# A two-stage kernel whose second stage gets its transposed rows by DMA, and whose first stage transposes the next tile one chunk earlier

## The chip, the cores and the metric

The kernel runs on one core of a Trainium2 chip. The metric is the time of one execution on the device, in microseconds (us). Five engines work side by side, each through its own queue of instructions in order: TensorE (PE: matmuls; its weight loads are listed as PEld), VectorE (DVE), ScalarE (ACT), GpSimd (POOL) and SyncE (SP). SyncE and ScalarE issue the transfers of this kernel, which 16 DMA engines carry out. Engines wait for each other by semaphores alone.

## What is computed

x has 2 x 1024 rows of 2048 values, ctx has 2 x 2048 rows of 2048 values.

```python
def fake_quant(x, s, z):                    # xattn: rounds to 0..255
    q = clip(round(x / s + z), 0, 255)
    return (q - z) * s
x = x + tanh(g_xattn) * matmul(fake_quant(layernorm(x)), fake_quant(ctx))      # per batch, 1024x2048 @ 2048x2048
y = layernorm(x)
logits = y @ gate_w.T + expert_bias         # 4 experts
one_hot = one_hot(argmax(logits))
z = y @ lora_A.T                            # 4 experts x 8
delta = z of the chosen expert @ lora_B.T
x = x + tanh(g_ffn) * (y @ W_up.T + delta)
```

## The kernel before

The 2048 rows are 16 tiles of 128 rows. A tile is 128 x 2048 in float32, 1 MB. Two stages follow each other on TensorE.

**First stage.** For each tile t: VectorE's `moments` (line 545) and `quant_scale`, ScalarE's `sqrt` (line 352), then ScalarE's `quant` rounds the normalised tile to int16 into one of two buffers `q1` in HL (line 358), and VectorE's `clip` (line 592) makes exact bfloat16 of it. TensorE transposes it in 16 blocks of 128 x 128 (`transposes`, line 853) into two PSUM banks TR, and ScalarE's `evac` copies both out to `q1T` (line 377); for tiles 0 to 3 VectorE copies the second half. Then come four chunks of 512 columns, each of 16 matmuls (`chunk`, line 875), and VectorE adds each chunk to the rows (`epi`, line 599). Tiles 0 to 3 go through chunk by chunk together, tiles 4 to 15 one by one. The transposes of tile t + 1 stand behind chunk 1 of tile t, that is its second. ctx arrives as 32 tiles; ScalarE rounds each (`ctx_round`, line 385), VectorE clips it (`ctx_clip`, line 609). Tiles 8 to 15 use ctx tiles 16 to 31.

The order of work on ScalarE and VectorE is written out by hand in `period(p, a, b, c)`, one call for each tile from 4 on. On ScalarE a period is: a, `sqrt(p + 2)`, b, `quant(p + 2)`, `evac(p + 1)`, c. In periods 4 to 7 the pieces a, b and c round one ctx tile each; from period 8 on they are absolute sums of a tile of W (`abs_sum`, line 394) and high halves of it (`w_high`, line 403). VectorE's period has `epi` of the last chunk of tile p - 1, `moments(p + 2)`, a, `epi`, `quant_scale(p + 2)`, `epi`, b, `clip(p + 2)`, `epi`, c. There, a, b and c are `ctx_clip`, later the powers of two of W (`w_pow`, line 617) and the low halves (`w_low`, line 629). SyncE's queue holds the loads and the stores in one written order: `store(t)` waits for `epi` of the last chunk of tile t, `row(u)` waits for the store that frees its buffer, and the loads of ctx and W wait for the buffers that they fill.

**Second stage.** W_up with the gates and lora_A beside it is 2084 columns wide and is kept in SBUF as two float16 halves; each row of it (a partition's columns of the k-th tile) is scaled by its own power of two. y, the normalised tile, is split into two float16 halves as well: VectorE's `norm` writes it in float32 to T (line 588), ScalarE's `y_high` rounds it to HL[:, 0] (line 413), and VectorE's `y_low` puts the rest in HL[:, 1] (line 636). HL holds one tile. TensorE transposes the two halves in 32 blocks, in four groups (`y_transposes`, line 912), VectorE multiplies each group by the column scales `wback` on its way out of PSUM into YT, the transposed tile, which has two buffers (`yT_out`, line 645). A tile's product (`tile2`) is five chunks of 416 to 418 columns, 48 matmuls each (line 920), with an addition for lora_B at the end of each (line 927) and a small transpose for z behind the second chunk (line 934). In the middle of tile s stand the transposes of tile s + 1: groups 0 and 1 ahead of chunk 3, groups 2 and 3 ahead of chunk 4. VectorE's order for a tile is `route(s)` (line 659 on), `moments`, `norm`, `y_low` of tile s + 1, then `epi2(s, c)` (line 693) with the four `yT_out` of tile s + 1 among them. ScalarE's is the store of tile s - 1 (line 424), `z_out(s)` (line 419), `sqrt` and `y_high` of tile s + 1. SyncE loads the rows that were put away in the first stage.

Of the kernel before, what the change touches and what calls it, by code (L numbers as in the profile page):

```python
# [7 lines left out]
ALU = mybir.AluOpType  # L8
# [3 lines left out]
P = 128  # L12
# [6 lines left out]
def build(nc, x, ctx, w, b_t, scal, out):  # L19
# [17 lines left out]
    KEEP = 4  # L37
    HALF = KT // 2
# [7 lines left out]
    o_t = out.rearrange("(t p) d -> t p d", p=P)  # L46
    h_t = nc.dram_tensor("h_scratch", (TILES - KEEP, P, D), F32).ap()

# [7 lines left out]
    with es:  # L56
# [12 lines left out]
        YT = sb("rows_T", [P, 2, KT, 2, P], F16)  # L69
# [4 lines left out]
        Braw = S1[0:ZR, 0:D]  # L74
        arena_bf = arena[:, :].bitcast(BF16)
        arena_i16 = arena[:, :].bitcast(I16)
        q1T = YT[:, :, :, :, :].rearrange("p a k h m -> p (a k h m)").bitcast(BF16).rearrange(
# [99 lines left out]
        s_yh = sem("y_high"); s_yl = sem("y_low"); s_yt = sem("yT_group"); s_ye = sem("yT_out")  # L177
        s_m2 = sem("chunk2_done"); s_dl = sem("delta_done"); s_rt = sem("route_step"); s_zs = sem("z_stack_ready")
# [36 lines left out]
        def _(sp):  # L215
# [111 lines left out]
            for s in range(KEEP + 1, TILES):  # L327
                row(TILES + s)
# [18 lines left out]
        def _(act):  # L347
# [57 lines left out]
            def y_high(s):  # L405
                act.wait_ge(s_norm, s + 1)
                if s == 0:
                    act.wait_ge(s_tr, 2 * TILES)
                else:
                    act.wait_ge(s_yt, 4 * s)  # L410
                    act.wait_ge(s_yl, s)
                u = TILES + s
                A(HL[:, 0, :], Xt(u), ACT.Identity, bias=L(u, "nmr"), scale=L(u, "rstd")).then_inc(s_yh, 1)  # L413
# [21 lines left out]
            ctx_round(0)  # L435
            evac(0)
            ctx_round(1)
            sqrt(1)
            ctx_round(2)
            quant(1)  # L440
# [25 lines left out]
            def period(p, a, b, c):  # L466
# [37 lines left out]
        def _(dve):  # L504
# [67 lines left out]
            def norm(s):  # L572
# [15 lines left out]
                v.tensor_scalar(T[:, 0:D], Xt(u), L(u, "mean"), L(u, "rstd"), ALU.subtract, ALU.mult).then_inc(s_norm, 1)  # L588
# [43 lines left out]
            def y_low(s):  # L632
                dve.wait_ge(s_yh, s + 1)
                if s >= 1:
                    dve.wait_ge(s_yt, 4 * s)
                v.tensor_tensor(HL[:, 1, :], T[:, 0:D], HL[:, 0, :], ALU.subtract).then_inc(s_yl, 1)  # L636

            def yT_out(s, g):
# [3 lines left out]
                src = TR[g % 2].bitcast(F16).rearrange("p (a m) -> p a m", a=4)  # L642
                dst = YT[:, s % 2, 4 * g:4 * g + 4].rearrange("p k h m -> p k (h m)")
                back = wc[:, 4 * g:4 * g + 4].unsqueeze(2).to_broadcast([P, 4, 2 * P])
# [152 lines left out]
            step(v.tensor_scalar(wc[:, :], wp[:, :], V["rPM"], None, ALU.mult))  # L797
            step(v.tensor_scalar(V["sc2"], V["PM"], UN, None, ALU.mult))
# [21 lines left out]
            for s in range(1, TILES):  # L820
# [5 lines left out]
                for c in range(3):  # L826
                    epi2(s, c)
                for g in range(4):
                    if g == 2:
                        epi2(s, 3)  # L830
                    if s + 1 < TILES:
                        yT_out(s + 1, g)
                epi2(s, 4)

        @block.tensor
        def _(pe):
# [46 lines left out]
            def stage1(slow):  # L883
# [19 lines left out]
            def y_transposes(s, g):  # L903
# [6 lines left out]
                for i in range(8):  # L910
                    k, h = 4 * g + i // 2, i % 2
# [4 lines left out]
            def products(s, c, kts, first):  # L916
                a, b = CUT[c], CUT[c + 1]
                for kt in kts:
                    for yh, wh in ((0, 0), (0, 1), (1, 0)):
                        mm = mmul(bank[c][:, 0:b - a], YT[:, s % 2, kt, yh, :], W(kt, wh, a, b),  # L920
# [18 lines left out]
            def tile2(s):  # L939
                nxt = s + 1 < TILES  # L940
                pe.wait_ge(s_ye, 4 * s + 4)
# [8 lines left out]
                if nxt:  # L950
                    y_transposes(s + 1, 0)
                    y_transposes(s + 1, 1)
# [3 lines left out]
                if nxt:  # L956
                    y_transposes(s + 1, 2)
                    y_transposes(s + 1, 3)
# [66 lines left out]
```

## Time and profile before

| what | value |
|---|---|
| median of 3 runs | 1028.18 us |
| runs | 1027.31 to 1029.14 us |
| profiled execution, its own time | 1028.02 us |
| its span, first to last instruction | 1026.2 us |
| TensorE busy | 972.0 us (95%) |
| VectorE busy | 460.6 us (45%) |
| ScalarE busy | 230.3 us (22%) |
| mean granted TensorE clock | 0.99 of full speed |

The span is the time between the first and the last instruction in the trace; the rest of the execution lies around it. Busy shares are averages over both stages. Matmuls are pipelined and their ends are modelled, so the distance between two starts is a better measure than the duration of a row.

### The profile page before, as it was taken

How to read it: one execution, taken by the hardware profiler on the slowest of the kernel's cores; microseconds unless marked ns; L12 is line 12 of the kernel's file. 1: busy time of each engine (PE TensorE's matmuls, PEld its weight loads, DVE VectorE, ACT ScalarE, POOL GpSimd, SP SyncE). 2: the span in 40 equal slices, each digit the busy share in tenths (PEclk: the TensorE clock that was granted, in tenths of full speed). 3: DMA queues.
4: the chain of work that ended last, by engine and by line, in shares of the span. 5: the costliest groups of instructions: out<-in, count | busy, mean ns of one | idle time of the engine just before them, and what ended most of it. 6: DMA issues, size and time to landing. Idle time of an engine off the chain costs nothing.

```text
span 1026.2 us, 13127 instructions
## 1 busy us (share of the span) xinstructions
PE 972.0 (95%) x5728; PEld 531.3 (52%) x5728; DVE 460.6 (45%) x885; ACT 230.3 (22%) x192; POOL 2.3 (0%) x16
## 2 busy tenths in 40 slices
PE   2899799899899999999999999999999999999997
PEld 1444344444355555555555555555555555555554
DVE  6764565766577542342534233252424325242401
ACT  6584657575633000000000000000000000000000
POOL 0000000000000000000000000000000000000000
PEclk9999999999899999999999999999999999999999
DMA  9968967677534202021020202112020210101011
GB/s 373 420 240 328 402 259 274 200 246 289 221 139 143 82 1 83 1 82 61 22 82 1 83 1 82 42 42 82 2 82 1 82 42 1 42 1 42 1 42 42
DMA packets 16445, 119.57 MB, mean 117 GB/s; under 512 B 1952, under 2 KB 1952, under 8 KB 1952
## 3 DMA queue, kind: packets, MB, share of 16 engines
q1 hardware_dynamic: 14080, 101.90, 26.1%
q10 hardware_dynamic: 2304, 16.78, 4.0%
q8 instruction: 48, 0.79, 0.3%
q14 instruction: 13, 0.11, 0.0%
HBM read 89.31 MB, written 29.36 MB: 116 GB/s over the span
## 4 chain that ended last, share of the span: by engine, by line
PE 74%; DMA 11%; ACT 5%; DVE 5%; issue 3%; SPq 1%; ACTq 0%; DVEq 0%
PE bank L920 62%; PE bank L875 7%; PE bank L912 3%; DMA arena<-in_ctx 2%; ACT arena L385 2%; DMA rows<-in_x 2%; DMA normed<-in_w 2%; DMA h_scratch<-rows 2%; DVE arena L629 2%; DMA stage<-in_ctx 1%; DMA stage<-in_w 1%; PE bank L927 1%; ACT rows_T L377 1%; DVE bn L545 1%; ACT halves L358 1%
## 5 line engine op out<-in xcount | busy, mean ns | idle before, releaser
L920 PE MATMUL bank<-arena,rows_T 128*128 128x416 f16 (+1 forms) x3840 | 686.6, 339 | 2.2 <-DVE arena L629 1.2
L920 PEld LDWEIGHTS bank<-arena,rows_T 128*128 128x128 f16 x3840 | 370.6, 97 | 300.5 <-issue 4.6
L875 PE MATMUL bank<-arena,rows_T 128*128 128x512 bf16 x1024 | 235.5, 390 | 30.2 <-ACT rows_T L377 18.4
L875 PEld LDWEIGHTS bank<-arena,rows_T 128*128 128x128 bf16 x1024 | 100.7, 100 | 157.6 <-issue 21.0
L693 DVE SCALAR_TENSOR_TENSOR rows<-bank,derived,rows 128x416 f32<-128x416 f32 (+2 forms) x80 | 48.4, 641 | 228.9 <-PE bank L927 228.9
L419 ACT ACTIVATE z_stack_T<-bank 96x128 fp32r<-96x128 f32 x16 | 4.4, 274 | 600.7 <-PE bank L934 600.7
L545 DVE BATCH_NORM_STATS2 bn<-rows 128x6 f32<-128x512 f32 x124 | 76.5, 680 | 10.7 <-DMA rows<-in_x 8.6
L645 DVE TENSOR_TENSOR rows_T<-bank,wback 128x1024 f16<-128x1024 f16 x64 | 75.0, 1216 | 0.2 <-DVE z_stack L675 0.2
L659 DVE SCALAR_TENSOR_TENSOR route<-bank,derived,scal 128x4 f32<-128x4 f32 x16 | 3.5, 221 | 115.9 <-PE bank L920 115.8
L599 DVE SCALAR_TENSOR_TENSOR rows<-bank,derived,rows 128x512 f32<-128x512 f32 x60 | 44.4, 747 | 20.9 <-PE bank L875 20.8
L636 DVE TENSOR_TENSOR halves<-normed,halves 128x2048 f16<-128x2048 f32 x16 | 36.7, 2292 | 30.3 <-ACT halves L413 30.3
L385 ACT ACTIVATE arena<-arena,scal,derived 128x2048 int16<-128x2048 f32 x22 | 45.2, 2084 | 10.2 <-DMA arena<-in_ctx 10.2
L413 ACT ACTIVATE halves<-rows,ln 128x2048 f16<-128x2048 f32 x16 | 33.5, 2095 | 39.7 <-DVE normed L588 39.7
L609 DVE TENSOR_SCALAR arena<-arena,derived 128x2048 bf16<-128x2048 int16 x32 | 24.0, 750 | 37.0 <-ACT arena L385 37.0
L554 DVE RECIPROCAL ln<-ln 128x1 f32<-128x1 f32 x32 | 5.1, 160 | 66.3 <-ACT ln L352 66.3
L912 PE MATMUL bank<-ident_h,halves 128*128 128x128 f16 x512 | 34.3, 220 | 0.2 <-DVE rows_T L645 0.2
L358 ACT ACTIVATE halves<-rows,ln 128x2048 int16<-128x2048 f32 x15 | 31.3, 2087 | 4.8 <-DVE ln L569 4.8
L912 PEld LDWEIGHTS bank<-ident_h,halves 128*128 128x128 f16 x512 | 29.0, 98 | 6.2 <-issue 5.0
L853 PE MATMUL bank<-ident_bf,halves 128*128 128x128 bf16 x256 | 17.7, 225 | 15.2 <-DVE halves L592 15.2
L629 DVE SCALAR_TENSOR_TENSOR arena<-stage,wscale,arena 128x2084 f16<-128x2084 f32 x11 | 26.1, 2384 | 8.3 <-ACT arena L403 8.2
L927 PE MATMUL bank<-b_stack,z_stack_T 96*128 96x416 f32 (+2 forms) x80 | 29.1, 432 | 0.4 <-ACT z_stack_T L419 0.4
L377 ACT ACTIVATE rows_T<-bank 128x1024 bf16<-128x1024 bf16 x28 | 27.1, 1010 | 8.9 <-PE bank L853 8.9
(82 smaller groups left out, 271.9 us busy)
## 6 DMA issues: line engine op xcount, KB each, us to landing
arena<-in_ctx SPq DMA_DIRECT2D x22, 1024.0 KB, 17.7
stage<-in_w SPq DMA_DIRECT2D x17, 1042.0 KB, 6.2
out<-rows ACTq DMA_DIRECT2D x16, 1024.0 KB, 3.9
rows<-in_x SPq DMA_DIRECT2D x15, 1024.0 KB, 9.9
rows<-h_scratch SPq DMA_DIRECT2D x12, 1024.0 KB, 4.8
h_scratch<-rows SPq DMA_DIRECT2D x11, 1024.0 KB, 8.3
stage<-in_ctx SPq DMA_DIRECT2D x10, 1024.0 KB, 10.4
normed<-in_w SPq DMA_DIRECT2D x7, 1042.0 KB, 6.6
```

What stands on the lines that cost most here:

```text
L358: A(q1_i16(t), Xt(t), ACT.Relu, bias=L(t, "qb"), scale=L(t, "qs")).then_inc(s_qi, 1)
L377: A(q1T[:, t % 4, GROUP * g:GROUP * (g + 1), :].rearrange("p k m -> p (k m)"), TR[g].bitcast(BF16), ACT.Copy).then_inc(s_ev, 1)
L385: A(Qc(c, True), buf, ACT.Relu, bias=z2, scale=V["rs2"]).then_inc(s_cr, 1)
L545: v.bn_stats(bn[:, u % 2, i, :], Xc(u, i * 512, (i + 1) * 512)).then_inc(s_bn, 1)
L599: v.scalar_tensor_tensor(out=xs, in0=bank[ROT[g % 6]][:, :], scalar=V["coef"], in1=xs, op0=ALU.mult, op1=ALU.add).then_inc(s_epi, 1)
L629: v.scalar_tensor_tensor(out=W(n, 1), in0=wbuf[k][:, :], scalar=wa[:, n:n + 1], in1=W(n, 0), op0=ALU.mult, op1=ALU.subtract).then_inc(s_lo, 1)
L645: v.tensor_tensor(dst, src, back, ALU.mult).then_inc(s_ye, 1)
L693: v.scalar_tensor_tensor(out=xs, in0=bank[c][:, a - CUT[c]:b - CUT[c]], scalar=V["gs"], in1=xs, op0=ALU.mult, op1=ALU.add).then_inc(s_e2, 1)
L875: mm = mmul(bk, q1T[:, t % 4, kt, :], Q(b, n, kt), start=(kt == 0), stop=(kt == KT - 1 and not slow), skip_group_check=slow)
L912: mm = nc.tensor.transpose(TR[g % 2].bitcast(F16)[:, i * P:(i + 1) * P], HL[:, h, k * P:(k + 1) * P], idh[:, :])
L920: mm = mmul(bank[c][:, 0:b - a], YT[:, s % 2, kt, yh, :], W(kt, wh, a, b), start=(first and kt == kts[0] and yh == 0 and wh == 0), stop=False,
L927: mmul(bank[c][:, a - CUT[c]:b - CUT[c]], zT[:, :].bitcast(F32R), Bst[:, a - EXT:b - EXT], start=False, stop=True, skip_group_check=True). ...
```

## The change

In the second stage tiles 0 and 1 (`BY_PE = 2`) keep TensorE's transposes. Tiles 2 to 15 are transposed by one DMA each, SBUF to SBUF, that SyncE issues: both halves of HL, 128 x 4096 float16, into YT, whose layout is now half, k, row. It waits for the low half of the tile and for the products of tile s - 2, which used the same half of YT. `y_high` of the tile after waits for this transfer instead of the transposes, since it overwrites HL. The column scales were applied on the way out of PSUM; now they are applied ahead of the split, by a row WR that holds all 2048 of them in every partition. SyncE writes the 128 x 16 scales `wback` to memory and loads them back to all partitions into S0. `norm` multiplies by WR in place of the row's rstd, which `y_high` and `y_low` multiply in. The loads of rows 5 on for this stage now alternate with the transfers in SyncE's queue.

In the first stage the transposes of tile t + 1 stand behind chunk 0 of tile t in place of chunk 1, for tiles from 4 on. ScalarE's period is: a, `sqrt(p + 2)`, `evac(p + 1)`, `quant(p + 2)`, b, c. In the head of the program `sqrt(1)` and `quant(1)` come one place earlier.

```diff
+            for s in range(BY_PE, TILES):
+                if s + 3 < TILES:
+                    row(TILES + s + 3)
+                sp.wait_ge(s_yl, s + 1)
+                sp.wait_ge(s_m2, 5 * (s - 1))
+                sp.dma_start_transpose(YT[:, s % 2].rearrange("p h k m -> p (h k) m"),
+                                       HL[:, :, :].rearrange("p h d -> p (h d)")).then_inc(s_dt, 16)
...
+            sp.wait_ge(s_wc, 1)
+            sp.dma_start(wrow_d.rearrange("k p -> p k"), wc[:, :],
+                         allow_slow_non_contiguous=True).then_inc(s_wr0, 16)
+            sp.wait_ge(s_wr0, 16)
+            sp.wait_ge(s_lo, KT)
+            sp.dma_start(WR, wrow_d.rearrange("k p -> (k p)").unsqueeze(0).to_broadcast([P, D])).then_inc(s_wr, 16)
...
-                b()
+                evac(p + 1)
                 if p + 2 < TILES:
                     quant(p + 2)
-                evac(p + 1)
+                b()
                 c()
...
+                    dve.wait_ge(s_wr, 16)
+                    v.scalar_tensor_tensor(out=T[:, 0:D], in0=Xt(u), scalar=L(u, "mean"), in1=WR, op0=ALU.subtract,
+                                           op1=ALU.mult).then_inc(s_norm, 1)
...
+                    v.scalar_tensor_tensor(out=HL[:, 1, :], in0=T[:, 0:D], scalar=L(TILES + s, "rstd"), in1=HL[:, 0, :],
+                                           op0=ALU.mult, op1=ALU.subtract).then_inc(s_yl, 1)
...
-                        if n == 1 and t + 1 < TILES:
+                        if n == 0 and t + 1 < TILES:
                             transposes(t + 1)
...
-                pe.wait_ge(s_ye, 4 * s + 4)
+                if s < BY_PE:
+                    pe.wait_ge(s_ye, 4 * s + 4)
+                else:
+                    pe.wait_ge(s_dt, 16 * (s - BY_PE + 1))
...
-                if nxt:
-                    y_transposes(s + 1, 0)
-                    y_transposes(s + 1, 1)
                 free2(s, 3)
```

TensorE's queue over one tile of the second stage, from its first chunk to the next tile's, stands like this before:

```order
L920 MATMUL bank<-arena,rows_T 128x416 x96
L934 MATMUL bank<-ident_f,z_stack 96x128
L920 MATMUL bank<-arena,rows_T 128x416 x48
L927 MATMUL bank<-b_stack,z_stack_T 128x380
L927 MATMUL bank<-b_stack,z_stack_T 128x416 x2
L912 MATMUL bank<-ident_h,halves 128x128 x16
L920 MATMUL bank<-arena,rows_T 128x418 x48
L927 MATMUL bank<-b_stack,z_stack_T 128x418
L912 MATMUL bank<-ident_h,halves 128x128 x16
L920 MATMUL bank<-arena,rows_T 128x418 x48
L927 MATMUL bank<-b_stack,z_stack_T 128x418
```

and like this after, where line 920 has become 946, 927 has become 953 and 934 has become 960:

```order
L946 MATMUL bank<-arena,rows_T 128x416 x96
L960 MATMUL bank<-ident_f,z_stack 96x128
L946 MATMUL bank<-arena,rows_T 128x416 x48
L953 MATMUL bank<-b_stack,z_stack_T 128x380
L953 MATMUL bank<-b_stack,z_stack_T 128x416 x2
L946 MATMUL bank<-arena,rows_T 128x418 x48
L953 MATMUL bank<-b_stack,z_stack_T 128x418
L946 MATMUL bank<-arena,rows_T 128x418 x48
L953 MATMUL bank<-b_stack,z_stack_T 128x418
```

Both blocks of 16 transposes are gone from the tile; nothing else moved. SyncE's queue behind the last load of W stands like this after the change (`stage1` is where B lands, `stage0` is WR):

```order
L331 DMA stage1<-in_b_t 96x2048
L333 DMA w_back_row<-wback 128x16x1
L337 DMA stage0<-w_back_row 128x2048
L229 DMA rows<-h_scratch 128x2048
L343 DMA_TRANSPOSE rows_T<-halves 128x32x128
```

Before, the load of B is followed by the loads of rows alone; now the two transfers of the scales stand between, and each load of rows but for the last ones is followed by one transposing transfer. In the first stage, ScalarE's queue from the copy of tile 5 (period 4) to that of tile 6 (period 5) stands like this before (`rows_T` is the copy out of PSUM, `arena` a ctx tile rounded, `ln` the square root, `halves` the x tile rounded; what is left out is a branch that isn't taken):

```order
L377 ACTIVATE rows_T<-bank 128x1024 x2
L385 ACTIVATE arena<-arena,scal,derived 128x2048 x2
L352 ACTIVATE ln<-ln 128x1
L385 ACTIVATE arena<-stage,scal,derived 128x2048
L358 ACTIVATE halves<-rows,ln 128x2048
...
L377 ACTIVATE rows_T<-bank 128x1024 x2
```

and after, with 377 become 393, 385 become 401, 352 become 368 and 358 become 374:

```order
L393 ACTIVATE rows_T<-bank 128x1024 x2
L374 ACTIVATE halves<-rows,ln 128x2048
...
L401 ACTIVATE arena<-stage,scal,derived 128x2048
L401 ACTIVATE arena<-arena,scal,derived 128x2048 x2
L368 ACTIVATE ln<-ln 128x1
L393 ACTIVATE rows_T<-bank 128x1024 x2
```

The copy of tile 6 stood behind the ctx tile of operation b (the one from `stage`) and the rounding of tile 7; now it is ahead of both.

## Rows read from the trace of the kernel before

**Rows 1.** The page's chain that ended last, shares of the span by line

```profile
PE bank L920 62%; PE bank L875 7%; PE bank L912 3%; DMA arena<-in_ctx 2%; ACT arena L385 2%; DMA rows<-in_x 2%; DMA normed<-in_w 2%; DMA h_scratch<-rows 2%; DVE arena L629 2%; DMA stage<-in_ctx 1%; DMA stage<-in_w 1%; PE bank L927 1%; ACT rows_T L377 1%; DVE bn L545 1%; ACT halves L358 1%
```

**Rows 2.** Timeline of one second-stage tile: start us, duration us, engine, line, operation, [idle before]

```profile
615.38 17.05 PE L920 MATMUL bank<-arena,rows_T 128*128 128x416 f16 x96
...
620.13 0.32 SPq L224 DMA_DIRECT2D rows<-h_scratch  x1
...
634.01 1.35 DVE L588 TENSOR_SCALAR normed<-rows,ln 128x2048 f32<-128x2048 f32 x1
...
637.52 2.29 DVE L636 TENSOR_TENSOR halves<-normed,halves 128x2048 f16<-128x2048 f32 x1 [2.16 <-ACT halves L413]
...
641.38 1.07 PE L912 MATMUL bank<-ident_h,halves 128*128 128x128 f16 x16
...
642.28 8.64 PE L920 MATMUL bank<-arena,rows_T 128*128 128x418 f16 x48
...
651.86 8.66 PE L920 MATMUL bank<-arena,rows_T 128*128 128x418 f16 x48
...
660.55 0.70 PE L920 MATMUL bank<-arena,rows_T 128*128 128x416 f16 x3
```

**Rows 3.** Timeline of TensorE in the last tile, fourth and fifth chunk

```profile
1002.71 8.65 PE L920 MATMUL bank<-arena,rows_T 128*128 128x418 f16 x48
...
1011.40 8.67 PE L920 MATMUL bank<-arena,rows_T 128*128 128x418 f16 x48
```

**Rows 4.** The page's groups: count | busy us, mean ns | idle before, releaser

```profile
L875 PE MATMUL bank<-arena,rows_T 128*128 128x512 bf16 x1024 | 235.5, 390 | 30.2 <-ACT rows_T L377 18.4 <-DVE arena L609 7.4 <-DVE rows_T L604 4.4
...
L629 DVE SCALAR_TENSOR_TENSOR arena<-stage,wscale,arena 128x2084 f16<-128x2084 f32 x11 | 26.1, 2384 | 8.3 <-ACT arena L403 8.2
```

**Rows 5.** Timeline of TensorE in the first stage

```profile
107.64 8.75 PE L875 MATMUL bank<-arena,rows_T 128*128 128x512 bf16 x32 [2.25 <-ACT rows_T L377]
...
127.42 8.75 PE L875 MATMUL bank<-arena,rows_T 128*128 128x512 bf16 x32 [3.23 <-ACT rows_T L377]
...
195.62 8.75 PE L875 MATMUL bank<-arena,rows_T 128*128 128x512 bf16 x32 [3.56 <-ACT rows_T L377]
...
262.37 9.88 PE L875 MATMUL bank<-arena,rows_T 128*128 128x512 bf16 x32 [4.05 <-ACT rows_T L377]
...
272.98 13.98 PE L875 MATMUL bank<-arena,rows_T 128*128 128x512 bf16 x64
```

**Rows 6.** DMA view: a queue's packets, MB, share; issues with KB and us to landing

```profile
q1 hardware_dynamic: 14080, 101.90, 26.1%
...
out<-rows ACTq DMA_DIRECT2D x16, 1024.0 KB, 3.9
...
rows<-h_scratch SPq DMA_DIRECT2D x12, 1024.0 KB, 4.8
...
scal<-in_scal SPq DMA_DIRECT2D x1, 5.0 KB, 1.6
```

**Rows 7.** Timeline: the load of B, and the high half of tile 2

```profile
324.77 0.34 SPq L326 DMA_DIRECT2D stage<-in_b_t  x1
...
364.38 2.10 ACT L413 ACTIVATE halves<-rows,ln 128x2048 f16<-128x2048 f32 x1 [2.44 <-DVE normed L588]
```

**Rows 8.** Timeline of ScalarE in the first stage

```profile
121.38 2.10 ACT L385 ACTIVATE arena<-stage,scal,derived 128x2048 int16<-128x2048 f32 x1 [5.20 <-DMA stage<-in_ctx]
...
125.36 1.91 ACT L377 ACTIVATE rows_T<-bank 128x1024 bf16<-128x1024 bf16 x2
...
139.61 2.10 ACT L385 ACTIVATE arena<-arena,scal,derived 128x2048 int16<-128x2048 f32 x1 [5.80 <-DMA arena<-in_ctx]
...
200.36 1.94 ACT L394 ACTIVATE arena<-stage 128x2084 f32<-128x2084 f32 x1 [2.96 <-DMA stage<-in_w]
...
235.46 1.94 ACT L394 ACTIVATE stage<-stage 128x2084 f32<-128x2084 f32 x1 [4.73 <-DMA stage<-in_w]
```

**Rows 9.** Chain that ended last, in order of time: start us, us, what

```profile
183.78 8.35 DMA h_scratch<-rows
```

More of the change, by code:

```diff
@@ L37, in build @@
     KEEP = 4
+    BY_PE = 2
     HALF = KT // 2
@@ L408, in y_high @@
                     act.wait_ge(s_tr, 2 * TILES)
-                else:
+                elif s <= BY_PE:
                     act.wait_ge(s_yt, 4 * s)
                     act.wait_ge(s_yl, s)
+                else:
+                    act.wait_ge(s_dt, 16 * (s - BY_PE))
                 u = TILES + s
-                A(HL[:, 0, :], Xt(u), ACT.Identity, bias=L(u, "nmr"), scale=L(u, "rstd")).then_inc(s_yh, 1)
+                if s < BY_PE:
+                    A(HL[:, 0, :], Xt(u), ACT.Identity, bias=L(u, "nmr"), scale=L(u, "rstd")).then_inc(s_yh, 1)
+                else:
+                    A(HL[:, 0, :], T[:, 0:D], ACT.Identity, scale=L(u, "rstd")).then_inc(s_yh, 1)
             def z_out(s):
@@ L587, in norm @@
                     dve.wait_ge(s_bst, 2)
-                v.tensor_scalar(T[:, 0:D], Xt(u), L(u, "mean"), L(u, "rstd"), ALU.subtract, ALU.mult).then_inc(s_norm, 1)
+                if s < BY_PE:
+                    v.tensor_scalar(T[:, 0:D], Xt(u), L(u, "mean"), L(u, "rstd"), ALU.subtract,
+                                    ALU.mult).then_inc(s_norm, 1)
+                else:
+                    dve.wait_ge(s_wr, 16)
+                    v.scalar_tensor_tensor(out=T[:, 0:D], in0=Xt(u), scalar=L(u, "mean"), in1=WR, op0=ALU.subtract,
+                                           op1=ALU.mult).then_inc(s_norm, 1)
             def clip(t):
@@ L633, in y_low @@
                 dve.wait_ge(s_yh, s + 1)
-                if s >= 1:
-                    dve.wait_ge(s_yt, 4 * s)
-                v.tensor_tensor(HL[:, 1, :], T[:, 0:D], HL[:, 0, :], ALU.subtract).then_inc(s_yl, 1)
+                if s < BY_PE:
+                    if s >= 1:
+                        dve.wait_ge(s_yt, 4 * s)
+                    v.tensor_tensor(HL[:, 1, :], T[:, 0:D], HL[:, 0, :], ALU.subtract).then_inc(s_yl, 1)
+                else:
+                    v.scalar_tensor_tensor(out=HL[:, 1, :], in0=T[:, 0:D], scalar=L(TILES + s, "rstd"), in1=HL[:, 0, :],
+                                           op0=ALU.mult, op1=ALU.subtract).then_inc(s_yl, 1)
             def yT_out(s, g):
@@ L641, in yT_out @@
                     dve.wait_ge(s_mm, place[(13 if s == 0 else 15, NCH - 1)] + 1)
-                src = TR[g % 2].bitcast(F16).rearrange("p (a m) -> p a m", a=4)
-                dst = YT[:, s % 2, 4 * g:4 * g + 4].rearrange("p k h m -> p k (h m)")
-                back = wc[:, 4 * g:4 * g + 4].unsqueeze(2).to_broadcast([P, 4, 2 * P])
+                src = TR[g % 2].bitcast(F16).rearrange("p (h a m) -> p h a m", h=2, a=4)
+                dst = YT[:, s % 2, :, 4 * g:4 * g + 4, :]
+                back = wc[:, 4 * g:4 * g + 4].unsqueeze(1).unsqueeze(3).to_broadcast([P, 2, 4, P])
                 v.tensor_tensor(dst, src, back, ALU.mult).then_inc(s_ye, 1)
@@ L825, in _ @@
                     y_low(s + 1)
-                for c in range(3):
+                for c in range(5):
                     epi2(s, c)
[L828 to L833, printed above, removed]
         @block.tensor
@@ L939, in tile2 @@
             def tile2(s):
-                nxt = s + 1 < TILES
-                pe.wait_ge(s_ye, 4 * s + 4)
+                if s < BY_PE:
+                    pe.wait_ge(s_ye, 4 * s + 4)
+                else:
+                    pe.wait_ge(s_dt, 16 * (s - BY_PE + 1))
                 for c in range(3):
```

22 lines of the change are left out of this document (11 added, 11 removed).

## The prediction

> **What bounds the kernel now.** I read the chain of waits first [rows 1]. Line 920, TensorE's products in the second stage, carries 62% of the span, and no other line more than 7. So I read that stage at the size of one tile [rows 2]: the first product of a tile starts at 615.38, that of the next at 660.55, 45.17 us later, and between them TensorE is never idle. Within the tile there are two blocks of 16 transposes (line 912). The next products start 0.90 us after each block does (641.38 to 642.28 for the first). The last tile has no such block [rows 3]: from its fourth chunk to its fifth 8.69 us pass (1002.71 to 1011.40), against 9.58 in [rows 2] (642.28 to 651.86), so a block costs 0.89 to 0.90 us of the path. The first stage is another matter [rows 4, 5]: TensorE sits idle for 30.2 us before line 875, 18.4 of them until line 377, ScalarE's copy of the transposes out of PSUM, in eight waits. [Rows 5] has the four longest, 2.25, 3.23, 3.56 and 4.05; the others are 1.68, 1.97, 0.16 and 1.55. Behind the four the next 32 matmuls take 8.75 us (three times) or 9.88, where half of the 64 in 13.98 us is 7.0, and 7.07 stands behind the shorter waits: the granted clock falls to the lower of its levels (1.2 of 2.4 GHz) for a while after such a wait. That adds 3 x 1.68 + 2.81 = 7.85 us. 18.4 + 7.85 = 26.3 us is thus all that a perfect first-stage order could return.
>
> **Second stage, what goes.** Tiles 2 to 15, 14 of them, are transposed by DMA; their 28 blocks leave TensorE: 28 x 0.90 = 25.2 us. VectorE loses its copies out of PSUM too, but it has idle time and doesn't set the end. Nothing else on TensorE's path changes, if the transposed tile has landed when the next tile starts.
>
> **Second stage, what comes.** That condition is the heart of the forecast. One buffer of halves holds the tile, so its transfer starts only after the low half (line 636), and must end before the next tile starts. In [rows 2] the low half starts at 637.52 and takes 2.29: it ends 639.81, 24.4 us into the tile. Two edits shift this. Line 588 becomes an operation with two tensor inputs, since it multiplies by the row of scales: line 629 does such an operation on 2084 columns in 2.38 us [rows 4], so 2048 take 2.34 where now 1.35 stand, 1.0 us more. The low half becomes the same kind, 2.34 instead of 2.29. So the transfer is released 25.5 us into a tile, and the tile lasts 45.17 - 1.80 = 43.37 us. The slack is 43.37 - 25.5 = 17.9 us. In SyncE's queue the load of rows for tile s + 3 is ahead of it, and waits for the store of tile s - 2. Such a load is issued at 620.13 in [rows 2], 4.8 us into the tile and as soon as the store has landed, so 20 us before the transfer is released. Both megabytes are through by then, and the transfer has the DMA engines to itself.
>
> How long it takes no row shows. Nearest by bytes are the loads and stores of 1 MB in this stage, 4.8 and 3.9 us [rows 6]. By pieces it could be far worse: the SP queue moved 14080 packets of 7.2 KB in 26.1% of 16 engines' time, 0.304 us each; a transposed megabyte falls into 32 blocks x 128 rows = 4096 pieces of 256 bytes, and if each cost as much as such a packet it would take 4096 x 0.304 / 16 = 78 us. The price lies between 4 and 78 us. I take it as under 17.9, because a plain megabyte needs 4.8 and the slack is 3.7 times that, while the piece bound charges 256 bytes like 7.2 KB. Then it costs nothing, and TensorE covers it. If the cover is gone, each microsecond above 17.9 is paid 14 times, as the release of the next transfer moves with the start of its tile.
>
> The Trainium skill, Advanced Engine Details and Errata, section X-Bar Transpose (TRN2), says that such transfers are as fast as plain ones, 350 to 400 GB/s: an estimate of 3 us for this megabyte, and the sum would be the same.
>
> **The row of scales.** The column scales go out to memory as 2048 single values and come back to all partitions. SyncE issues both behind the load of B, which it issues at 324.77, and the first user is the norm of tile 2, just before the high half at 364.38 [rows 7]: both moments move alike. That is 39 us for two transfers. If each of the 2048 values cost a packet's 0.304 us the first would take 39 us and the second some 5, a lateness of 5 us that the slack of tile 2 mostly takes. I take zero, 0 to 5.
>
> **First stage.** On TensorE the transposes of tile t + 1 come one chunk earlier; on ScalarE their copy comes ahead of rounding the next x tile (line 358) and of operation b of the period. Up to tile 8 operation b rounds a ctx tile that has just landed. [Rows 8] show the present order: b starts at 121.38, when its load has landed, rounding follows it, the copy is third at 125.36, and TensorE starts at 127.42 [rows 5]. Each of the next loads waits for a store of the tile before, so this is a loop. Landings in it are at 121.38 and 139.61, 18.2 us apart. The two operations that come out of it from behind b, 2.0 for rounding (as for b, 125.36 - 121.38 for both) and 1.9 for the copy, leave 18.2 - 3.9 = 14.3, less than TensorE's own tile: four chunks in 13.98 [rows 5] and 0.90 for the transposes, 14.9 us. So for tiles 5 to 8 TensorE becomes the bound, and the waits before them go: 2.25 + 3.23 + 1.68 + 1.97 = 9.1 us and 2 x 1.68 of slow clock, 12.5. One comes back: the transposes asked for earlier need the x tile rounded and clipped, and VectorE clips it behind b. That is about 1.4 us before tile 7's (b lands at 121.4, is rounded and clipped by 124.3; TensorE would be ready about 123). Gain 11.1 us.
>
> From tile 9 on ScalarE works on W, and another loop rules: a load of W has landed at 200.36, the corresponding one two tiles later at 235.46 [rows 8], 35.1 us for two tiles where TensorE needs 29.8. In it are rounding, copy, high half and absolute sums, VectorE's clip, moments and low half, and on SyncE a store, the load of the next row tile that waits for it, and a load of W behind that. The store alone takes 8.35 us [rows 9]. The change only permutes ScalarE's share, so the loop keeps its 35 us. The 9.3 us of waits from tile 10 on stay, in other places: the copy is earlier, but TensorE asks for transposes whose x tile isn't clipped yet. Only before tile 14 (the wait of 4.05), where operation a has the late load, does the copy no longer stand behind b and rounding, 4 us; the high half on which that load depends now stands 4 us later itself and takes most of it back. I add 1, and get 12 us for the stage, between 5 (half of the first part) and 20 (most of 26.3). The head of the program changes order too, but its first chunks wait for ctx tiles that VectorE clips behind the moments of a late row tile, in either order: zero.
>
> **Sum.** The profiled execution took 1028.02 us, of which 1026.2 are its span; the median shown is 1028.18, so nothing has to be shifted. 1028.0 - 25.2 - 12 = 991 us.
>
> **Rivals.**
> - *The transposing transfer outlasts its slack.* Against it stand 4.8 us per plain megabyte; for it, that a transfer in pieces of 256 bytes has no row here. The place is TensorE's wait at the start of tiles 2 to 15; the time is 1028.0 - 25.2 - 12 + 14 x (D - 17.9), D being the transfer. It beats the old kernel up to D = 20.6 and is slower beyond: at 30 us it gives 1160, at the piece bound of 78 about 1830. A form of it: the 32 blocks of 128 x 128 go one after another, each at the 1.6 us of the smallest transfer here [rows 6], 51 us in all; 991 + 14 x 33.3 = 1457 us, with a chance of 0.08 of its own. I give D over 20.6 a chance of 0.20 with it, 17.9 to 20.6 one of 0.04. The Trainium skill, VectorE: DVE Perf Modes, section The three transpose paths, prices such a block by DMA at 1309 ns, by which 32 in a row would be an estimate of 42 us and 1327 us in all; no row of this trace shows which of the skill's two pages holds.
> - *The first stage gains nothing* (or loses up to 5), because its DMA engines are already full in the slices before tile 8 and earlier demand only makes transfers longer, or because the earlier transposes wait for VectorE's clip each time. For it: the store of 8.35 us in [rows 9] takes twice the 3.9 of the second stage [rows 6]. Then 1028.0 - 25.2 = 1003, up to 1008. Chance 0.11.
> - *The change's transfer disturbs TensorE's reads* or moves the start of tile 2 by the row of scales: below 5 us, inside the range.
>
> **Chances.** Transfer hidden and first stage gaining 5 to 20 us: 0.65, 991 us, own range 983 to 998. First stage without gain: 0.11. Transfer a little too long but still a win: 0.04. Slower: 0.20. The range must leave out no more than 0.2: it goes from 980 to 1040, which holds some 0.02 of the slow case (D up to 21.4) and nearly all of the rest. The measurement tells 0.2% (2 us) from no change: faster 0.79, the same 0.01, slower 0.20.
>
> **What would show it.** In the profile after: DMA_TRANSPOSE rows with a time from issue to landing; under 18 us the step holds. A tile of the second stage should last 43.4 us and TensorE show no wait at its first product; a wait there for a DMA is the first rival. The low half should end about 25.5 us into the tile. In the first stage tile 9's first product should come some 11 us earlier, the waits for ScalarE's copy before tiles 5 to 8 be gone, some 8 us of waits remain between tiles 10 and 15, now partly ahead of the transposes, and line 920 start about 12 us earlier. The forecast is wrong if the transfer is slow, or if the W loop of the first stage is shorter in the new order than I say.

## The result and the profile after

The changed kernel takes 992.62 us (992.0 to 995.08, 4 runs) where the kernel before takes 1027.94 us (1027.31 to 1029.14, 4 runs). The ratio is 0.966, 95% interval 0.9641 to 0.9678: 35 us less. Its profiled execution spans 991.1 us, before 1026.2. The forecast was 991.

The page's chain that ended last, as in [rows 1], has TensorE's products of the second stage (now line 946) at 64%, and those of the first stage (now 901) at 13% instead of 7%. TensorE sets the pace of the first stage for longer:

```profile
PE 80%; DMA 8%; DVE 5%; ACT 4%; issue 2%; SPq 1%; ACTq 0%; DVEq 0%
PE bank L946 64%; PE bank L901 13%; DMA stage<-in_w 2%; DVE arena L656 2%; ACT arena L401 2%; DMA rows<-in_x 2%; DMA arena<-in_ctx 2%; PE bank L953 2%; ACT arena L419 1%; DMA h_scratch<-rows 1%; DMA stage<-in_ctx 1%; DVE bn L566 1%; PE bank L879 1%; DMA stage<-in_b_t 1%; DMA normed<-in_w 1%
```

One tile of the second stage in the timeline after, to be read against [rows 2] (start us, duration us, engine, line, operation, idle before):

```profile
594.56 17.05 PE L946 MATMUL bank<-arena,rows_T 128*128 128x416 f16 x96
...
613.19 2.35 DVE L614 SCALAR_TENSOR_TENSOR normed<-rows,ln,stage 128x2048 f32<-128x2048 f32 x1
615.58 2.00 ACT L434 ACTIVATE halves<-normed,ln 128x2048 f16<-128x2048 f32 x1 [3.45 <-DVE normed L614]
617.61 2.35 DVE L666 SCALAR_TENSOR_TENSOR halves<-normed,ln,halves 128x2048 f16<-128x2048 f32 x1 [2.07 <-ACT halves L434]
...
619.99 4.87 SPq L343 DMA_TRANSPOSE rows_T<-halves  x1
...
637.94 17.05 PE L946 MATMUL bank<-arena,rows_T 128*128 128x416 f16 x96
```

The tile lasts 637.94 - 594.56 = 43.38 us, 1.79 less than before, and TensorE doesn't wait at its start. The low half ends at 619.96, 25.4 us into the tile, and SyncE issues the transfer at once. The DMA view (as [rows 6]) has the quantity that no row of before could show:

```profile
q1 hardware_dynamic: 74080, 117.64, 35.4%
...
stage<-w_back_row SPq DMA_DIRECT2D x1, 1024.0 KB, 5.2
stage<-in_b_t SPq DMA_DIRECT2D x1, 768.0 KB, 7.2
rows_T<-halves SPq DMA_TRANSPOSE x14, 6.7
...
w_back_row<-wback SPq DMA_DIRECT2D x1, 8.0 KB, 12.0
```

A transposing transfer of 1 MB lands 6.7 us after its issue (the middle of 14; the first of them took 8.5). This one is in flight from 619.99 to about 626.7, with 11 us to spare.

TensorE in the first stage, the waits of the timeline (as [rows 5]) and the start of the second stage:

```profile
127.44 1.07 PE L879 MATMUL bank<-ident_bf,halves 128*128 128x128 bf16 x16 [1.30 <-DVE halves L619]
...
203.89 1.07 PE L879 MATMUL bank<-ident_bf,halves 128*128 128x128 bf16 x16 [2.75 <-DVE halves L619]
...
220.61 1.07 PE L879 MATMUL bank<-ident_bf,halves 128*128 128x128 bf16 x16 [1.84 <-DVE halves L619]
...
238.79 1.34 PE L879 MATMUL bank<-ident_bf,halves 128*128 128x128 bf16 x16 [3.29 <-DVE halves L619]
...
253.79 3.61 PE L901 MATMUL bank<-arena,rows_T 128*128 128x512 bf16 x16 [1.90 <-DVE rows L626]
...
285.21 29.25 PE L946 MATMUL bank<-arena,rows_T 128*128 128x416 f16 x165 [0.96 <-issue]
```

The waits for ScalarE's copy are gone. The second stage starts at 285.21; before it was 296.61, so 11.4 us came from the first stage. From there to the end of the span it is 705.9 us, before 729.6: 23.7 us from the second. What is left of the waits from tile 4 on is VectorE's clip (line 619), ahead of the transposes, and one wait for an `epi` (line 626).

ScalarE in the same stretch, against [rows 8]:

```profile
118.54 1.92 ACT L393 ACTIVATE rows_T<-bank 128x1024 bf16<-128x1024 bf16 x2
...
123.83 2.09 ACT L401 ACTIVATE arena<-stage,scal,derived 128x2048 int16<-128x2048 f32 x1 [0.56 <-DMA stage<-in_ctx]
...
191.43 1.94 ACT L410 ACTIVATE arena<-stage 128x2084 f32<-128x2084 f32 x1 [6.34 <-DMA stage<-in_w]
...
227.79 1.94 ACT L410 ACTIVATE stage<-stage 128x2084 f32<-128x2084 f32 x1 [7.12 <-DMA stage<-in_w]
```

The copy of tile 6 now runs at 118.54, ahead of operation b at 123.83, where before it was behind it at 125.36. The two landings of W that the forecast named are 36.4 us apart (191.43 to 227.79), before 35.1: this loop has not become shorter.

### The profile page after: what moved, and what is told of

Read it like the earlier page. It is cut to its first block, busy times and chain, and to the rows that moved or that the text cites. A ratio compares the mean times of both kernels' runs of the same rounds, so it can differ in the third digit from the quotient of the medians.

```text
span 991.1 us, 12169 instructions
## 1 busy us (share of the span) xinstructions
PE 941.7 (95%) x5256; PEld 505.6 (51%) x5280; DVE 411.8 (42%) x829; ACT 229.4 (23%) x192; POOL 2.3 (0%) x16
## 3 DMA queue, kind: packets, MB, share of 16 engines
q1 hardware_dynamic: 74080, 117.64, 35.4%
## 4 chain that ended last, share of the span: by engine, by line
PE 80%; DMA 8%; DVE 5%; ACT 4%; issue 2%; SPq 1%; ACTq 0%; DVEq 0%
PE bank L946 64%; PE bank L901 13%; DMA stage<-in_w 2%; DVE arena L656 2%; ACT arena L401 2%; DMA rows<-in_x 2%; DMA arena<-in_ctx 2%; PE bank L953 2%; ACT arena L419 1%; DMA h_scratch<-rows 1%; DMA stage<-in_ctx 1%; DVE bn L566 1%; PE bank L879 1%; DMA stage<-in_b_t 1%; DMA normed<-in_w 1%
## 5 line engine op out<-in xcount | busy, mean ns | idle before, releaser
L901 PE MATMUL bank<-arena,rows_T 128*128 128x512 bf16 x1000 | 227.9, 386 | 14.7 <-issue 4.8
L666 DVE SCALAR_TENSOR_TENSOR halves<-normed,ln,halves 128x2048 f16<-128x2048 f32 x14 | 32.9, 2351 | 29.0 <-ACT halves L434 29.0
L434 ACT ACTIVATE halves<-normed,ln 128x2048 f16<-128x2048 f32 x14 | 28.0, 2002 | 48.6 <-DVE normed L614 48.6
L614 DVE SCALAR_TENSOR_TENSOR normed<-rows,ln,stage 128x2048 f32<-128x2048 f32 x14 | 32.9, 2351 | 0.8 <-DVE ln L599 0.4
L879 PEld LDWEIGHTS bank<-ident_bf,halves 128*128 128x128 bf16 x256 | 16.0, 102 | 29.6 <-issue 15.3
L419 ACT ACTIVATE arena<-stage,wscale 128x2084 f16<-128x2084 f32 x11 | 22.1, 2022 | 15.8 <-PE bank L901 11.8
```

Source lines behind the costliest of these rows:

```text
L419: A(W(n, 0), wbuf[k][:, :], ACT.Identity, scale=wa[:, n:n + 1]).then_inc(s_hi, 1)
L614: v.scalar_tensor_tensor(out=T[:, 0:D], in0=Xt(u), scalar=L(u, "mean"), in1=WR, op0=ALU.subtract, op1=ALU.mult).then_inc(s_norm, 1)
L666: v.scalar_tensor_tensor(out=HL[:, 1, :], in0=T[:, 0:D], scalar=L(TILES + s, "rstd"), in1=HL[:, 0, :], op0=ALU.mult, op1=ALU.subtract).the ...
L879: mm = nc.tensor.transpose(TR[g].bitcast(BF16)[:, i * P:(i + 1) * P], q1(t)[:, k * P:(k + 1) * P], idb[:, :])
L901: mm = mmul(bk, q1T[:, t % 4, kt, :], Q(b, n, kt), start=(kt == 0), stop=(kt == KT - 1 and not slow), skip_group_check=slow)
```

## The experiments

Each kernel is the changed one with the edit shown, unless it says otherwise. Ratios are to the kernel before, run beside it on the same chip.

**The two halves, each alone.** `dma_only` undoes the first-stage edits, and the new order of the head as in `head_back` below:

```diff
-                evac(p + 1)
+                b()
                 if p + 2 < TILES:
                     quant(p + 2)
-                b()
+                evac(p + 1)
...
-                        if n == 0 and t + 1 < TILES:
+                        if n == 1 and t + 1 < TILES:
```

> The second-stage part of the change alone; the first stage is in the order of before (transposes behind the second chunk, copy behind operation b and rounding, old head). Theory: the two parts add up, and the second stage is worth the 23.7 us that line 946 starts nearer to the end of the span (1026.2 - 296.6 before, 991.1 - 285.2 after), so about 1004 us. Rival: the first stage's new order only moved waits that are given back later, so this kernel gives 993 us like the whole change.

Measured: 1006.23 us, ratio 0.9788 (0.9763 to 0.9813), 20.9 us under the 1027.12 of before. That is 2.8 us less than the 23.7 expected; 2.0 of them lie in tile 0 of the second stage, which took 51.1 us here and 49.1 in the profile after, for the cause shown below under the scales. Its waits for the copy are back, with the slow matmuls behind them (timeline of TensorE):

```profile
109.27 8.73 PE L901 MATMUL bank<-arena,rows_T 128*128 128x512 bf16 x32 [2.29 <-ACT rows_T L393]
...
129.28 8.76 PE L901 MATMUL bank<-arena,rows_T 128*128 128x512 bf16 x31 [3.49 <-ACT rows_T L393]
```

`first_only` is the kernel before with the first-stage edits alone, those of the head included.

> The first-stage part alone; the second stage has TensorE's transposes for all tiles. Theory: 11.4 us, the amount by which the second stage starts earlier in the profile after (296.6 to 285.2), so about 1016.5 us. Rival: the gain needs the second stage's change, and this gives 1026 to 1028 us.

Measured: 1015.04 us, ratio 0.9879 (0.9856 to 0.9902), 12.1 us less. 20.9 + 12.1 = 33.0, and the whole change measured 34 to 35 us: the halves add up, and neither rival holds.

**Which first-stage edit carries the gain.** `early_transposes` keeps the transposes behind chunk 0 and puts ScalarE's period back:

```diff
-                evac(p + 1)
+                b()
                 if p + 2 < TILES:
                     quant(p + 2)
-                b()
+                evac(p + 1)
```

> The whole change, but ScalarE's period in the old order (a, sqrt, b, quant, copy, c); only TensorE's transposes are one chunk earlier. Theory: the copy still stands behind the load that b waits for, so TensorE waits before tiles 5 to 8 as before; the first stage gains at most 1 us and the time is about 1003 us. Rival: the earlier transposes carry the gain, 993 us.

Measured: 1007.0 us, ratio 0.9797 (0.9766 to 0.9827), the same as `dma_only`. TensorE still waits before tile 6 as in [rows 5]:

```profile
130.41 3.61 PE L901 MATMUL bank<-arena,rows_T 128*128 128x512 bf16 x16 [3.26 <-ACT rows_T L393]
```

`copy_first` is the other half:

```diff
-                        if n == 0 and t + 1 < TILES:
+                        if n == 1 and t + 1 < TILES:
```

> The whole change, but TensorE's transposes stay behind the second chunk; only ScalarE's copy is ahead of rounding and b. Theory: ScalarE's queue now waits 3.5 us longer per tile for the transposes, with b and rounding behind it, so the W loop gets longer and part of the gain is lost: 995 to 1003 us. Rival: the copy's place is all that matters, 993 us or less, since VectorE's clip no longer stops the transposes (11 us of waits in the profile after).

Measured: 994.67 us, ratio 0.967 (0.9644 to 0.9696), not to be told from the whole change (0.966), nor from the 994.31 us of `transfer_x2`, which was run beside it with the transposes early. The time lies just under the theory's 995 to 1003 and above the rival's 993, but the mechanism of the theory is not there: the two landings of W that it would have moved apart (191.73 and 228.18) are 36.5 us apart, against 36.4 in the profile after. The place of the copy in ScalarE's queue is all of the gain that can be measured; moving the transposes adds at most 2 us. With the transposes late the clip stops TensorE less, but two long waits for line 626 stand in its place, one of them this:

```profile
253.95 8.53 PE L901 MATMUL bank<-arena,rows_T 128*128 128x512 bf16 x31 [5.13 <-DVE rows L626]
```

**Is the rest of the waits a loop or a place?** `clip_first` takes away what the transposes wait for:

```diff
-                b()
                 if p + 2 < TILES:
                     clip(p + 2)
+                b()
```

> The whole change, and on VectorE the clip of tile p + 2 moves ahead of operation b of the period. It takes away what TensorE's transposes wait for in the profile after (1.30, 2.75, 1.84 and 3.29 us, for line 619). Theory: from tile 9 on the loop through SyncE's store, row load, load of W and back through ScalarE and VectorE sets the pace (36.4 us for two tiles in the profile after: 191.43 to 227.79), and the waits only move to another place of that loop; only the 1.3 us before tile 7's transposes, in the ctx part, can be won: 991 to 993 us. Rival: each wait is a cost of its own, caused by the clip's place behind b; then 9.2 us go, 983.5 us.

Measured: 992.73 us, ratio 0.9667 (0.9643 to 0.969); the changed kernel beside it (`after_again`) 993.64 us, 0.9665 (0.9646 to 0.9684). No difference. In its timeline of TensorE no wait for the clip is left, and these have come:

```profile
209.20 3.61 PE L901 MATMUL bank<-arena,rows_T 128*128 128x512 bf16 x16 [0.61 <-ACT rows_T L393]
...
227.52 0.93 PE L901 MATMUL bank<-arena,rows_T 128*128 128x512 bf16 x2 [3.34 <-DVE rows L626]
...
249.26 6.41 PE L901 MATMUL bank<-arena,rows_T 128*128 128x512 bf16 x16 [5.19 <-DVE rows L626]
```

From tile 9 on 0.61 + 3.34 + 5.19 = 9.1 us of waits stand against 9.8 in the profile after (the 1.90 for line 626 counted). The 1.30 us before tile 7's transposes and a wait of 0.25 before tile 6's are gone. Where the last wait ends is set by the loop and not by the clip: TensorE starts tile 14 at 253.79 in the profile after and at 249.26 here, and both are 4.1 us behind the same landing of W (in `after_again` too, 253.37 behind 249.28), which is

```profile
249.69 1.94 ACT L410 ACTIVATE stage<-stage 128x2084 f32<-128x2084 f32 x1 [3.44 <-DMA stage<-in_w]
```

in the profile after, and 245.17 here. But the loop does not have a fixed length. Here the landings that were 36.4 us apart are at

```profile
189.09 1.94 ACT L410 ACTIVATE arena<-stage 128x2084 f32<-128x2084 f32 x1 [6.43 <-DMA stage<-in_w]
...
223.43 1.94 ACT L410 ACTIVATE stage<-stage 128x2084 f32<-128x2084 f32 x1 [5.75 <-DMA stage<-in_w]
```

34.3 us apart; in `scales_early` below, which leaves the clip where it was, they are 34.9 apart, so how much of this is the clip's stays open. Counted from the end of TensorE's last wait for a ctx tile (66.74 in the profile after, 64.83 here), tile 14 starts 2.6 us earlier. The granted clock takes that back: behind the wait of 5.19 us 16 matmuls take 6.41 us (granted clock 0.54), behind the one of 1.90 they take 3.61. So the waits are no costs of their own that add up to 9.2 us, as the rival has it; whether the clip's place is worth 1 or 2 us these runs don't show. `after_again`:

> The changed kernel itself, beside the three that follow, so that differences below 0.3% can be read within one call: 992.6 us, within 1.5.

**How much room the transfer has.** `transfer_x2` and `transfer_x3` repeat each transposing transfer, one behind the other; the waits on `s_dt` count all of them. Shown is `transfer_x3`; in `transfer_x2` the two threes are twos:

```diff
-                sp.dma_start_transpose(YT[:, s % 2].rearrange("p h k m -> p (h k) m"),
-                                       HL[:, :, :].rearrange("p h d -> p (h d)")).then_inc(s_dt, 16)
+                for r in range(3):
+                    if r:
+                        sp.wait_ge(s_dt, 16 * (3 * (s - BY_PE) + r))
+                    sp.dma_start_transpose(YT[:, s % 2].rearrange("p h k m -> p (h k) m"),
+                                           HL[:, :, :].rearrange("p h d -> p (h d)")).then_inc(s_dt, 16)
```

> The whole change, with each transposing transfer made twice, the second when the first has landed, so D = 2 x 6.7 = 13.5 us. Theory: the slack is 17.9 us (637.94 - 619.99 in the profile after), so nothing moves: 992.6 us. Rival: D counts from the first microsecond, through SyncE's queue or the SBUF ports: 14 x 6.7 = 94 us more, 1087 us.

Measured: 994.31 us, ratio 0.9664 (0.9636 to 0.9693). Doubling the transfer costs nothing: in its trace TensorE waits for none of the 14, and each of their tiles lasts 43.38 us as in the profile after.

> The same three times over, D = 3 x 6.7 + 0.2 = 20.3 us. Theory: 2.4 us beyond the slack, paid 14 times: 992.6 + 34 = 1026 us, with a wait of 2.4 us on TensorE at the start of each tile from 2 on. Rival: the clock falls behind each of these waits, as it did in the first stage, and adds up to 1.7 us a tile: 1050 us. Second rival: the slack is larger than the rows say, 993 us.

Measured: 1067.79 us, ratio 1.04 (1.0361 to 1.0439), 73.5 us above `transfer_x2`, which was run beside it; all three theories were short. The chain of waits shows two tiles of it, three transfers each, and the timeline of TensorE what stands behind:

```profile
558.19 6.72 DMA rows_T<-halves
...
564.93 8.30 DMA rows_T<-halves
...
573.25 8.08 DMA rows_T<-halves
...
608.74 6.71 DMA rows_T<-halves
...
615.47 6.71 DMA rows_T<-halves
...
622.19 6.74 DMA rows_T<-halves
```

```profile
581.37 19.00 PE L949 MATMUL bank<-arena,rows_T 128*128 128x416 f16 x96 [5.05 <-DMA rows_T<-halves]
...
628.98 18.74 PE L949 MATMUL bank<-arena,rows_T 128*128 128x416 f16 x96 [2.12 <-DMA rows_T<-halves]
```

In the second of these tiles D is 628.93 - 608.74 = 20.2 us and TensorE waits 2.12: the slack is 18.1 us, where the forecast had 17.9. What the first theory missed is in two parts. In five of the 14 tiles one or two transfers took 8 us or more, so the waits sum to 47.3 us, not 14 x 2.4 = 34. Some of these long ones ran beside a store of ScalarE's queue (573.25 to 581.33, with the store issued at 577.05), others beside none (564.93 to 573.23); their cause is open. And in 12 of 14 tiles the next 96 products take more than 17.05 us, mostly 18.7: the granted clock is 0.59 over the 4 us behind the wait in the second tile above, and 21 us are lost in all, which only the rival had foreseen. In the two others it doesn't fall (waits of 2.12 and 2.14 us, products in 17.05). From tile 1 to the end of the span `transfer_x3` takes 727.4 us and `transfer_x2` 656.8; 47.3 + 21 = 68 of these 70.7 us are thus found.

**The scales beside the load of B.** Before, one group of tile 1's transposes waits for line 645, for 0.22 us:

```profile
339.39 0.62 PE L912 MATMUL bank<-ident_h,halves 128*128 128x128 f16 x8 [0.22 <-DVE rows_T L645]
```

After, two groups wait for it (now line 676):

```profile
328.16 0.62 PE L938 MATMUL bank<-ident_h,halves 128*128 128x128 f16 x8 [1.56 <-DVE rows_T L676]
329.29 0.62 PE L938 MATMUL bank<-ident_h,halves 128*128 128x128 f16 x8 [0.51 <-DVE rows_T L676]
```

`scales_early` moves the write of the scales to a place where SyncE waits anyway:

```diff
-            for i in range(KT + 2, KT + 8):
+            load_w(KT + 2)
+            sp.wait_ge(s_wc, 1)
+            sp.dma_start(wrow_d.rearrange("k p -> p k"), wc[:, :],
+                         allow_slow_non_contiguous=True).then_inc(s_wr0, 16)
+            for i in range(KT + 3, KT + 8):
                 load_w(i)
```

> The whole change, but the write of the 2048 scales is issued 37 us earlier, behind the load of W tile 10 (second pass), where SyncE waits for the buffers of W anyway. Theory: the 12 us write beside the load of B is what made that load land in 7.2 us instead of 5.1, which came back as the 1.56 and 0.51 us that TensorE waits for line 676; then B lands in 5.1 us and the time falls by 1.5 to 991.1 us. Rival: those waits come from line 676's new layout or from something else, and the time stays at 992.6; or the write now slows the last loads of W and costs up to 3 us.

Measured: 991.8 us, ratio 0.9655 (0.963 to 0.9679), beside 993.24 us, 0.9663, of `head_back`. Once more, as `scales_early_again`:

> The early write of the scales alone, once more beside the changed kernel. Theory: 1 to 1.5 us under it. Rival: 0, within the spread of the executions.

Measured: 991.01 us, ratio 0.9644 (0.9625 to 0.9663), beside 993.64 us of `after_again`. B's load and the first wait in this execution:

```profile
stage<-in_b_t SPq DMA_DIRECT2D x1, 768.0 KB, 5.9
```

```profile
326.27 0.62 PE L939 MATMUL bank<-ident_h,halves 128*128 128x128 f16 x8 [0.33 <-DVE rows_T L677]
```

B lands in 5.9 instead of 7.2 us and the first wait falls from 1.56 to 0.33, as the theory says; it doesn't fall to 5.1, and the second wait of 0.51 stays, so that one has another cause. VectorE works on B before it comes to line 676, so a later B moves it. The 14 traces show the size better than the times do. Tile 0 of the second stage, from its first product to that of tile 1, in us:

| the write of the scales | executions | B lands in | first wait for line 676 | tile 0 |
|---|---|---|---|---|
| none | `before`, `first_only` | 5.1, 5.1 | none | 47.8, 48.1 |
| beside the load of B | nine (the changed kernel twice) | 7.2 to 8.4 | 1.6 to 2.8 in eight, none in `after_again` | 49.1 to 52.4, the middle one 51.0 |
| earlier | `scales_early`, `scales_early_again`, `clip_first_scales_early` | 5.7, 5.9, 6.0 | none, 0.33, 0.43 | 47.6, 47.7, 48.6 |

In the eight the wait is B's landing time less 5.6 us, to within 0.1, and so it is in the two of the last row that wait. In `after_again` TensorE was late itself, by a wait of 1.99 us for a tile of W and slow matmuls behind it. The table shows the mechanism, and that the profile after, with 49.1 us, is the cheapest of the nine: the write beside B costs tile 0 from 1.3 to 4.6 us, the middle one 3, with slow matmuls behind the wait in the dearer ones, and the early write takes nearly all of it back. The medians differ by 1.4 and 2.6 us with the same sign; their intervals overlap.

`clip_first_scales_early` has both edits:

> clip_first with the early write of the scales. Theory: 1 to 1.5 us under clip_first, since TensorE's waits for line 676 (2.1 us in the profile after) go and nothing else stands on that place. Rival: no difference.

Measured: 990.04 us (988.16 to 992.45), ratio 0.9634 (0.9613 to 0.9656), the lowest median of the study. It is 2.7 us under `clip_first`, where 1 to 1.5 were expected, 1.0 under `scales_early_again` and 3.6 (0.4%) under the changed kernel beside it. It leaves nothing out and so beats the kernel before; against the changed one the intervals just overlap (0.9613 to 0.9656, 0.9646 to 0.9684).

**The head.** In the profile after, one chunk of the head took 5.30 us instead of 3.61; with 0.5 us that it was already late TensorE was 2.2 us behind before from there on. `head_back` restores the old order of the head:

```diff
-            sqrt(1)
             evac(0)
             ctx_round(1)
-            quant(1)
+            sqrt(1)
             ctx_round(2)
+            quant(1)
```

> The whole change, but with sqrt(1) and quant(1) at their old places in ScalarE's head. In the profile after, tile 0's last chunk before tile 3's transposes took 5.30 us instead of 3.61 and TensorE was 2.2 us later from there on. Theory A: the new head order costs this, so 990.5 us. Theory B: the granted clock behind a wait of 2.6 us falls in some executions and not in others, whatever the order; then the time stays at 992.6 us, within 0.5.

Measured: 993.24 us, ratio 0.9663 (0.9639 to 0.9686). Theory B holds. The same chunk in `head_back`, with the old head, and in `scales_early`, with the new one (two fences, timeline of TensorE):

```profile
38.45 5.30 PE L901 MATMUL bank<-arena,rows_T 128*128 128x512 bf16 x16 [2.63 <-DVE rows_T L631]
```

```profile
38.50 3.61 PE L902 MATMUL bank<-arena,rows_T 128*128 128x512 bf16 x16 [2.63 <-DVE rows_T L632]
```

The wait is the same to a hundredth, the order is not what decides, and the chunk takes 5.30 or 3.61 us. The granted clock from 37 to 43 us is 0.72 in the first of them and 1.00 in the second. The changed kernel itself had 5.30 in one execution and 3.61 in the other (`after_again`, behind a wait of 2.23).

## Why the prediction was right

The forecast of 991 us stands against 992.6 (profiled span 991.1), and its steps can be checked one by one. The mechanisms of both parts are the forecast's; that the sum is so close owes something to small terms of opposite sign, named below.

- **The price of TensorE's transposes.** 28 blocks at 0.90 us, 25.2 us. Measured by the tile: 14 x 1.79 = 25.1 us. Right.
- **Moment and slack of the transfer.** Low half done 25.5 us into the tile, slack 17.9 us. Measured 25.4, and 18.1 by `transfer_x3`. Line 588 in its new form takes 2.35 us, forecast 2.34. Right.
- **The transfer itself.** Bounds of 4 and 78 us, taken as under 17.9. Measured 6.7, so the value lay at the low end. No row had shown it: the forecast leaned on the plain megabyte and gave 0.24 to the rest, and this one guess decided between a gain and a loss. The bound by pieces was right in the count and wrong in the price: in the DMA view packets rise from 14080 to 74080, some 4100 for each transfer beside the 2048 of the scales, and the time of the queue from 0.261 x 16 x 1026.2 = 4285 us to 0.354 x 16 x 991.1 = 5614, so 60000 packets added 1329 us, by this estimate 0.022 us each (those of the scales are among them) and not 0.304. Neither of the two pages of the Trainium skill named in the prediction fits: the section X-Bar Transpose (TRN2) made it an estimate of 3 us, less than half of what was measured, and The three transpose paths, taken block by block, 42 us, six times as much.
- **The rival's formula.** 14 x (D - 17.9) was too cheap. It left out the granted clock, which fell behind 12 of 14 waits in `transfer_x3` and added 1.5 us a tile on average (21 / 14). A tile there with D = 20.2 loses 2.12 us of waiting and mostly 1.7 of clock, 3.8 us, and 14 of these are 53 us, more than the 35 gained. So the change would have been a loss from a D below 20.2 on, not from 20.6; how far below no run shows, since behind the waits of 1.55 to 1.97 us in the kernel before the matmuls were not slow. The main case isn't touched by it.
- **The row of scales.** Taken as 0 in a range of 0 to 5. This term was mis-sized: the write of 2048 single values took 12.0 us, not the 39 of its bound, but it ran beside the load of B, on which VectorE's path to line 645 depends. That cost was looked for at the norm of tile 2, the first user of the row, and it came in tile 0, from the queue's other transfer. In the profile after it is 1.3 us (tile 0 lasts 49.1 us, before 47.8), nearly the whole difference between 25.1 and the 23.7 measured; over nine executions it is 1.3 to 4.6.
- **First stage, the head.** Taken as zero, measured 2.2 us later than before (81.43 instead of 79.28 at the transposes of tile 4): 1.7 of them are the slow chunk, which comes in some executions and not in others. By `head_back` that is bad luck and no effect of the order; the other 0.5 stays open.
- **First stage, tiles 5 to 8.** 11.1 us, with one wait of 1.4 us left before the transposes of tile 7. Measured there: 1.30. The forecast wanted tile 9's first product some 11 us earlier. The transposes of tile 10 stand two chunks of 3.45 us behind it before and one after:

```profile
184.10 1.06 PE L853 MATMUL bank<-ident_bf,halves 128*128 128x128 bf16 x16
```

```profile
171.56 1.06 PE L879 MATMUL bank<-ident_bf,halves 128*128 128x128 bf16 x16
```

So that product is at 177.2 before and 168.1 after, 9.1 us earlier; with the 2.2 lost in the head these tiles won 11.2. Right, mechanism included: the copy before operation b, TensorE as the bound.

- **First stage, tiles 9 to 15.** The waits were to stay, in other places, with 1 us won. They did stay: 2.75, 1.84, 3.29 and 1.90 us, 9.8 against 9.3, and the loop is 36.4 us instead of 35.1. The gain was 2.3 us, and it came from the granted clock: slow matmuls behind the waits cost 1.68 + 2.81 = 4.5 us before and 1.7 after. The forecast had this cost in its list but took none of it back here. `clip_first` shows the last wait ending 4.1 us behind a landing of W wherever the clip stands; it doesn't show a loop of fixed length.
- **The stage in sum.** -2.2 + 11.2 + 2.3 = 11.3, measured 11.4, forecast 12: the head's loss and the unforeseen gain of the last tiles nearly cancel.
- **What the prediction gave to two edits together** is one edit's: the earlier transposes alone bring nothing, and the copy alone all that can be measured. The prediction didn't separate them, so its sum wasn't hurt.

## What to carry to other kernels

A transfer that replaces work of the bounding engine is worth that work as long as it fits between the release of its source and the first use of its target: measure this slack in the trace and compare it with the transfer's duration, not with the DMA engines' load. In a queue that runs in order, a copy that the bounding engine waits for belongs ahead of whatever waits for a load. Where a wait is part of a loop through several queues, removing what it names may only move it; compare the distance between two landings in the loop before and after to see whether anything was won, and look at the granted clock behind the wait that is left. A small transfer added to a queue is to be priced at what runs beside it as well as at its own first user.

## What the runs showed of the hardware

- A transposing DMA, SBUF to SBUF, of 128 x 4096 float16 lands in 6.7 us in most cases (14 of them from 6.7 to 8.5, and 42 from 6.7 to 9.6), against 4.8 for a plain load of the same size. The 8.5 is the first transfer of the kernel, with no other transfer beside it, and it came again in `transfer_x2` and `transfer_x3`. The row of its issue in SyncE's queue lasts 4.8 us, that of a plain transfer 0.33.
- A write of 2048 single float32 values takes 12 us for 8 KB, more than the 4.8 us of a plain megabyte, and with it a load of 768 KB beside it takes 7.2 to 8.4 us instead of 5.1.
- Behind a wait of 2.63 us of TensorE the same 16 matmuls took 3.61 us in some executions and 5.30 in others. In these runs the granted clock may or may not fall behind waits between 2.1 and 2.7 us; each fall costs about 1.7 us of matmuls.
